# Macaron block with a blocked tanh scan: four scan steps issued elsewhere, the first normalisation and the add of eps on VectorE, one wait fewer

## The chip, the cores and the metric

The kernel runs on one core of a Trainium2 chip. The metric is the device time of one execution in microseconds (us); the time before is the median of three runs. A row of the trace names its engine as PE (TensorE matmuls), PEld (TensorE weight loads), DVE (VectorE), ACT (ScalarE), POOL (GpSimd) or SP (SyncE, which only issues DMAs here); a "q" behind it (PEldq, POOLq) is that engine's sequencer, which handles waits and register arithmetic. Ln is line n of the kernel.

## The reference: what is computed

The input x is 8 sequences of 512 tokens with 128 features. Half a feed-forward block is added, then a scan, then half the same feed-forward block again:

```python
def _L0_ffn_ref(x, ...):                        # hidden width 512
    h = silu(_tlin(x, w1_w, w1_s)) * _tlin(x, w2_w, w2_s)
    h = gelu(_tlin(h, h1_w, h1_s))
    h = gelu(_tlin(h, h2_w, h2_s))
    return _tlin(h, w3_w, w3_s)
...
def _L0_attn_ref(x, A, B, C, W_out, b_out):
    xB = einsum('bsd,dn->sbn', x, B)            # 16 states
    step: h = tanh(xb_t + h @ A.T)              # 512 steps in order
    return einsum('sbn,nd->bsd', hs, C) @ W_out.T + b_out
...
x = x + 0.5 * _L0_ffn_ref(_layernorm(x), ...)
x = x + _L0_attn_ref(_layernorm(x), ...)
x = x + 0.5 * _L0_ffn_ref(_layernorm(x), ...)
```

`_layernorm` subtracts the mean over the features and divides by sqrt(variance + 1e-5).

## The kernel before

**Tiling.** The 4096 tokens are cut into 8 chunks of 512 columns. Each chunk goes through the feed-forward block twice, so there are 16 passes, numbered g = 0 to 15. A pass has four layers; layer 2 and layer 3 are 512 by 512. Each float32 operand that moves through TensorE is split into a high part and a low part (`y_hi`, `y_lo`), so that each product is two matmuls of 128x512 with the same weights. Layer 2 and layer 3 have four output tiles m, each summed over four k: eight matmuls each.

**The scan.** The 512 steps of a sequence are done as 8 blocks side by side, so a chunk carries 8 steps t = 0 to 7 for 32 columns. One step is a short loop over three engines: TensorE does one matmul of 128x32 (`scan_step` of the tensor block, L437, which reads the state `h`), ScalarE does two tanh (L1232, L1233), and VectorE takes the low part of the state (`scan_low`, L856), which releases the next step's matmul through the semaphore `step_h`.

**The turns.** One turn does layer 2, 3 and 4 of pass g, layer 1 of pass g + 1, and the eight scan steps of another chunk between them. There are four kinds: the first turn (g = 0), early turns (g = 1 to 5, with steps from g = 3), middle turns (g = 6 to 8, in which the steps stand closer together in the second half) and turns (g = 9 to 14; 9 to 13 with steps), then a last turn. Passes 4 and 5 and passes 10 to 13 run in loops, so that their waits compare with registers (the order of instructions shows such register work as REGISTER_ALU or ISA). In the trace the early turn 2 lies at 59 to 83 us, the middle turn 6 at 152 to 175, 7 and 8 at 175 to 223, turn 9 at 223 to 246 and the turns 10 to 13 at 246 to 336.

**The order.** Every engine's order of instructions is written out by hand, in five blocks of code, one for each engine. An engine goes through its own list strictly in order and waits for semaphores of the others. Nothing is scheduled by a tool.

**The statistics.** For every chunk VectorE computes mean and variance (`statistics`: four BN_STATS, a small MEMSET, four BN_AGGR into `mv_f` or `mv_m`). GpSimd then adds eps (`ve_f`, `ve_m`, L1481) and raises the sum to the power -0.5 (`rs_f`, `rs_m`, L1484), both in `inverse_std`. Then the tokens are normalised, four instructions of 128x128 each, by VectorE (`normalise`, L796, into `xnt_f` or `xnt_m`) or, in early turns, by ScalarE from `rs_f` and `nbias`. TensorE turns the result round with four transposes (`to_features`, L302). "f" is the normalisation in front of a feed-forward block, "m" that in front of the scan.

In a turn, VectorE's order around the change is: `attention` (writes `lnin`), `low1`, `front_stats`, `layer4` (L851, writes `x1c` in the first eight passes and `outb` in the later ones), step 0, step 1, `normalise`, `low` of layer 2, step 2. In the middle turns 7 and 8 `layer4` is followed by `normalise`, `middle_stats` and `low`, and TensorE reads `x1c` in `middle_tokens` (L282) between layer 2's m = 1 and m = 2.

**Waits.** `wait(pe, l4_out, g)` in `layer2` at m = 2 protects the bank that layer 4 used. `middle_tokens`, which stands ahead of it in early and middle turns, waits for `l4_out` to reach `mid + 1`, which is g in those turns.

Of the kernel before, what the change touches and what calls it, by code (L numbers as in the profile page):

```python
# [24 lines left out]
ALU = mybir.AluOpType  # L25
# [33 lines left out]
def build(nc, xT, xtok, w1T, w2T, h1T, h2T, w3T, scales, Ablk, Brep, CTrep, WoutT, ident_d, mask_d, outT):  # L59
    with ExitStack() as ctx:  # L60
# [208 lines left out]
        def _(pe):  # L269
# [67 lines left out]
            def layer2(g, m, gen, beside=lambda k: None, ks=range(KT)):  # L337
                if m == 0 and ks[0] == 0:
                    if isinstance(g, int) and g == 1:
                        pe.wait_ge(y3_hi_r, 1)  # L340
                    else:
                        pe.wait_ge(y1_r, 4 * g + 3)
                if m == 1:
                    wait(pe, y3_hi_r, 4 * g)
                if m == 2:
                    wait(pe, l4_out, g)
                for k in ks:
                    if m == 0:
                        pe.wait_ge(y1_hi_r[k], g + 1)
                        if k < KT - 1:  # L350
                            pe.wait_ge(y1_lo_r, (KT - 1) * g + k + 1)
                        else:
                            pe.wait_ge(y1_lo_last, g + 1)
                    mm = split_mm(B2[m][:, :], 2, k, m, y1_hi[:, k, :], y1_lo[:, k, :], k == 0, k == KT - 1, gen)
                    if k == KT - 1:
                        mm.then_inc(l2_mm, 1)
                    beside(k)
# [90 lines left out]
            def early_turn(g, gen, mid, scan):  # L448
# [17 lines left out]
                layer2(g, 2, gen)  # L466
# [7 lines left out]
                layer3(g, 0, gen)  # L474
                step(5)
# [156 lines left out]
            def turn(k, g, gen, att, scan, joined=True):  # L632
# [15 lines left out]
                step(1)  # L648
                layer2(g, 2, gen)
                step(2)  # L650
                to_features("f", xnt_f, FR, g + 1)
                layer2(g, 3, gen)
                step(3)
# [106 lines left out]
        def _(dve):  # L760
            def statistics(kind, g, tile, st, mv):
                for q in range(QT):
                    i = nc.vector.bn_stats(st[:, q, :], tile[:, q * P:(q + 1) * P])
                i.then_inc(bns[kind], 1)
                dve.wait_ge(bns[kind], g + 1)
                nc.vector.memset(spare[:, :], 0.0)
                for q in range(QT):
                    i = nc.vector.bn_aggr(mv[:, q, :], st[:, q, :])  # L768
                i.then_inc(var[kind], 1)

# [228 lines left out]
            def turn(k, g, att, scan, joined=True):  # L999
# [9 lines left out]
                step(0)  # L1009
                step(1)  # L1010
                normalise("f", g + 1, FR, mv_f, rs_f, xnt_f)
# [63 lines left out]
            i.then_inc(var["f"], 1)  # L1075
            dve.wait_ge(ld_sc, 16)
# [401 lines left out]
        def _(pool):  # L1478
            def inverse_std(kind, g, mv, ve, rs):
                pool.wait_ge(var[kind], g + 1)  # L1480
                pool.tensor_tensor(ve[:, :], mv[:, :, 1], epsc[:, :], ALU.add).then_inc(veps[kind], 1)  # L1481
                pool.wait_ge(veps[kind], g + 1)
                wait(pool, normed[kind], g)
                pool.tensor_tensor(rs[:, :], ve[:, :], mhalf[:, :], ALU.pow).then_inc(rstd[kind], 1)  # L1484
# [22 lines left out]
            def early_turn(g, mid):  # L1507
                inverse_std("f", g + 2, mv_f, ve_f, rs_f)
                bias(g + 2)
                inverse_std("m", mid, mv_m, ve_m, rs_m)  # L1510
                rest(g, True)

            def middle_turn(g, c):
                if c > 0:
                    inverse_std("f", g + 1, mv_f, ve_f, rs_f)
                inverse_std("m", g - 1, mv_m, ve_m, rs_m)
                rest(g, True)

            def turn(k, g):
                last = isinstance(k, int) and k == CHUNKS - 1  # L1520
                if not last:
                    inverse_std("f", g + 1, mv_f, ve_f, rs_f)
# [13 lines left out]
            inverse_std("f", 0, mv_f, ve_f, rs_f)  # L1536
# [8 lines left out]
            inverse_std("f", 1, mv_f, ve_f, rs_f)  # L1545
# [9 lines left out]
            inverse_std("f", 2, mv_f, ve_f, rs_f)  # L1555
# [12 lines left out]
            def round_(r):  # L1568
# [3 lines left out]
                else:  # L1572
                    inverse_std("f", gb + CHUNKS, mv_f, ve_f, rs_f)
# [108 lines left out]
```

## Time and profile before

| | |
|---|---|
| median of 3 runs | 384.46 us (384.4 to 384.72) |
| the profiled execution's own time | 385.06 us |
| its span, first to last instruction | 383.1 us |
| TensorE matmul busy | 376.4 us, 98% of the span, 1793 matmuls |
| TensorE weight loads busy | 300.2 us, 78% |
| VectorE busy | 279.7 us, 73% |
| ScalarE busy | 268.0 us, 70% |
| GpSimd busy | 163.9 us, 43% |
| granted TensorE clock | 1.000 over the whole span (the 2.4 GHz level) |
| DMA | 14.00 MB in the whole span |

The profiled execution took 0.60 us more than the median of the runs, and 1.96 us of it lie outside the span. The ends of matmuls are modelled in the profile, and neighbouring matmuls overlap in it; how fast TensorE really goes is read from the distance between the starts of neighbouring matmuls, and a late one is seen at its weight load, which in regular flow starts with the matmul ahead of it.

### The profile page before, as it was taken

How to read it: one execution, taken by the hardware profiler on the slowest of the kernel's cores; microseconds unless marked ns; L12 is line 12 of the kernel's file. 1: busy time of each engine (PE TensorE's matmuls, PEld its weight loads, DVE VectorE, ACT ScalarE, POOL GpSimd, SP SyncE). 2: the span in 40 equal slices, each digit the busy share in tenths (PEclk: the TensorE clock that was granted, in tenths of full speed). 3: DMA queues.
4: the chain of work that ended last, by engine and by line, in shares of the span. 5: the costliest groups of instructions: out<-in, count | busy, mean ns of one | idle time of the engine just before them, and what ended most of it. 6: DMA issues, size and time to landing. Idle time of an engine off the chain costs nothing.

```text
span 383.1 us, 6587 instructions
## 1 busy us (share of the span) xinstructions
PE 376.4 (98%) x1793; PEld 300.2 (78%) x1793; DVE 279.7 (73%) x724; ACT 268.0 (70%) x625; POOL 163.9 (43%) x156
## 2 busy tenths in 40 slices
PE   8999999999999999999999999999999999999995
PEld 6777777778878787878778788888888888887774
DVE  4878989896777677576868866776767677686713
ACT  3889595777858688576784767758576775757654
POOL 3555262655525355142551633525334352533421
PEclk9999999999999999999999999999999999999999
DMA  7920000000000000000001001010100101000001
GB/s 226 436 110 1 27 2 27 3 2 28 2 28 0 2 27 0 28 2 28 27 2 56 2 8 49 0 55 2 41 14 0 55 0 55 0 30 26 2 28 32
DMA packets 6365, 14.00 MB, mean 37 GB/s; under 512 B 1088, under 2 KB 2112, under 8 KB 6080
## 3 DMA queue, kind: packets, MB, share of 16 engines
q1 hardware_dynamic: 5328, 13.37, 9.1%
q10 hardware_dynamic: 1008, 0.29, 0.3%
q8 instruction: 12, 0.20, 0.2%
q14 instruction: 17, 0.14, 0.1%
HBM read 7.37 MB, written 2.10 MB: 25 GB/s over the span
## 4 chain that ended last, share of the span: by engine, by line
PE 85%; issue 7%; POOL 3%; ACT 3%; DVE 2%; POOLq 0%; DVEq 0%
PE F L274 66%; PE FR L274 7%; PE SC L491 2%; PE FR L302 2%; POOL y_lo L1489 1%; PE SC L422 1%; POOL y_lo L1495 1%; PE F L519 1%; ACT y_hi L1216 1%; PE FR L292 1%; PE SC L274 1%; PE MI L302 1%; ACT y L1213 1%; PE F L521 1%; PE MI L282 1%
## 5 line engine op out<-in xcount | busy, mean ns | idle before, releaser
L274 PE MATMUL F<-y_hi,w_hi 128*128 128x512 f32 (+1 forms) x484 | 196.6, 407 | 0.3 <-DVE y_lo L1045 0.2
L274 PE MATMUL F<-y_lo,w_hi 128*128 128x512 f32 (+1 forms) x484 | 188.6, 390 | 0.0
L274 PEld LDWEIGHTS F<-y_hi,w_hi 128*128 128x128 f32 x484 | 90.9, 188 | 20.7 <-issue 2.2
L1213 ACT ACTIVATE y<-F,sc 128x512 f32<-128x512 f32 x111 | 76.1, 686 | 41.3 <-PE F L274 40.1
L274 PEld LDWEIGHTS F<-y_lo,w_hi 128*128 128x128 f32 x484 | 91.2, 188 | 15.9
L837 DVE TENSOR_TENSOR y_lo<-y,y_hi 128x512 fp32r<-128x512 f32 x79 | 64.8, 821 | 39.2 <-ACT y_hi L1216 39.2
L1489 POOL TENSOR_TENSOR y_lo<-y,y_hi 128x512 fp32r<-128x512 f32 x48 | 66.7, 1398 | 59.1 <-DVE y_hi L824 48.5
L1495 POOL TENSOR_TENSOR y_lo<-y,y_hi 128x512 fp32r<-128x512 f32 x48 | 62.6, 1310 | 34.6 <-ACT y_hi L1216 34.4
L1216 ACT ACTIVATE y_hi<-F,sc 128x512 fp32r<-128x512 f32 x111 | 76.1, 685 | 0.0
L1232 ACT ACTIVATE h<-SC 128x32 fp32r<-128x32 f32 x96 | 18.8, 196 | 48.0 <-PE SC L437 46.8
L274 PE MATMUL F<-xn_hi,w_hi 128*128 128x512 f32 x118 | 49.5, 419 | 0.1
L807 DVE SCALAR_TENSOR_TENSOR u<-th,F 128x512 f32<-128x512 f32 x61 | 41.5, 681 | 7.0 <-ACT th L1195 7.0
L274 PE MATMUL F<-xn_lo,w_hi 128*128 128x512 f32 x118 | 46.3, 393 | 0.0
L1481 POOL TENSOR_TENSOR ve_f<-mv_f,epsc 128x4 f32<-128x4 f32 x16 | 3.2, 202 | 96.6 <-DVE mv_f L768 91.6
L817 DVE SCALAR_TENSOR_TENSOR y<-F,s12h,u 128x512 f32<-128x512 f32 x58 | 43.3, 747 | 1.6
L1195 ACT ACTIVATE th<-F,s1h 128x512 f32<-128x512 f32 x61 | 41.1, 689 | 3.2 <-PE F L274 2.4
L856 DVE TENSOR_TENSOR h<-SC,h 64x32 fp32r<-64x32 f32 x96 | 17.1, 178 | 19.0 <-ACT SC L1233 18.2
L274 PEld LDWEIGHTS F<-xn_hi,w_hi 128*128 128x128 f32 x118 | 22.1, 187 | 6.9 <-DVE y L817 1.3
L274 PEld LDWEIGHTS F<-xn_lo,w_hi 128*128 128x128 f32 x118 | 22.2, 189 | 3.4
L274 PE MATMUL FR<-y_hi,w_hi 128*128 128x512 f32 x60 | 24.0, 399 | 0.0
L274 PE MATMUL FR<-y_lo,w_hi 128*128 128x512 f32 x60 | 23.4, 390 | 0.0
L437 PEld LDWEIGHTS SC<-h,a_mix 128*128 128x128 f32 x95 | 17.8, 188 | 6.6 <-DVE h L856 2.9
(170 smaller groups left out, 439.6 us busy)
## 6 DMA issues: line engine op xcount, KB each, us to landing
x_all<-in_xT SPq DMA_DIRECT2D x1, 2048.0 KB, 16.1
x_all<-x1c SPq DMA_DIRECT2D x8, 256.0 KB, 2.3
x_all<-lnin SPq DMA_DIRECT2D x8, 256.0 KB, 2.2
out<-outb SPq DMA_DIRECT2D x7, 256.0 KB, 2.0
x_all<-in_xtok SPq DMA_DIRECT2D x1, 1536.0 KB, 12.0
w_raw<-in_h1T SPq DMA_DIRECT2D x2, 512.0 KB, 7.8
w_raw<-in_h2T SPq DMA_DIRECT2D x2, 512.0 KB, 9.3
x_all<-in_xtok SPq DMA_DIRECT2D x2, 128.0 KB, 3.2
```

The costliest lines, as they stand in the source:

```text
L274: mm = nc.tensor.matmul(out, wtile(w, layer, k, m), y, start=first and i == 0, stop=last and i == len(pairs) - 1)
L437: nc.tensor.matmul(SC[:, span(t)], a_mix[:, :], states, start=False, stop=True, skip_group_check=True).then_inc(step_mm, 1)
L807: nc.vector.scalar_tensor_tensor(out=u[:, m % 2, :], in0=th[:, m % 2, :], scalar=1.0, in1=l1_banks(g, m, late)[0][:, :], op0=ALU.add, op1= ...
L817: nc.vector.scalar_tensor_tensor(out=y1[:, m, :], in0=l1_banks(g, m, late)[1][:, :], scalar=s12h[:, m:m + 1], in1=u[:, m % 2, :], op0=ALU. ...
L837: nc.vector.tensor_tensor(y_lo[:, k, :], y[:, k, :], y_hi[:, k, :].bitcast(F32), ALU.subtract).then_inc(out_sem, 1)
L856: nc.vector.tensor_tensor(h[0:64, span(t)], SC[0:64, span(CSTEPS + t)], h[0:64, span(t)].bitcast(F32), ALU.subtract).then_inc(step_h, 1)
L1195: nc.scalar.activation(th[:, m % 2, :], l1_banks(g, m, late)[0][:, :], ACT.Tanh, scale=s1h[:, m:m + 1]).then_inc(th_r, 1)
L1213: nc.scalar.activation(y23[:, m, :], bankt[:, :], ACT.Gelu, scale=s)
L1216: nc.scalar.activation(y_hi[:, m, :], bankt[:, :], ACT.Gelu, scale=s).then_inc(hi_r, 1)
L1232: nc.scalar.activation(h[:, span(t)], SC[:, span(t)], ACT.Tanh)
L1489: pool.tensor_tensor(y1_lo[:, m, :], y1[:, m, :], y1_hi[:, m, :].bitcast(F32), ALU.subtract).then_inc(y1_lo_r if m < KT - 1 else y1_lo_las ...
L1495: pool.tensor_tensor(y_lo[:, k, :], y[:, k, :], y_hi[:, k, :].bitcast(F32), ALU.subtract).then_inc(out_sem, 1)
```

## The change

Five edits, with nothing changed in what is computed:

1. On TensorE, step 1 of a turn is issued after the first k of layer 2's tile m = 2 instead of ahead of that tile; step 3 after the third k of tile m = 3 instead of behind the tile.
2. On TensorE, step 5 of an early turn is issued after the third k of layer 3's first tile instead of behind it.
3. On VectorE, a turn's `normalise` stands between step 0 and step 1 instead of behind step 1.
4. VectorE adds eps itself at the end of `statistics`, for every chunk and both kinds; it waits for its own BN_AGGR (`var`) and for the last use of the old value (`rstd`). GpSimd's `inverse_std` only raises to the power.
5. In early turns the wait for `l4_out` in `layer2` at m = 2 is left out.

The four scan steps or stages that stand elsewhere are thus steps 1 and 3 of `turn` and step 5 of `early_turn` on TensorE, and step 1's states against the normalisation on VectorE.

```diff
@@ tensor block
-            def layer2(g, m, gen, beside=lambda k: None, ks=range(KT)):
+            def layer2(g, m, gen, beside=lambda k: None, ks=range(KT), taken=True):
...
-                if m == 2:
+                if m == 2 and taken:
                     wait(pe, l4_out, g)
@@ tensor block, early_turn
-                layer2(g, 2, gen)
+                layer2(g, 2, gen, taken=False)
...
-                layer3(g, 0, gen)
-                step(5)
+                layer3(g, 0, gen, lambda k: step(5) if k == 2 else None)
@@ tensor block, turn
-                step(1)
-                layer2(g, 2, gen)
+                layer2(g, 2, gen, lambda i: step(1) if i == 0 else None)
                 step(2)
                 to_features("f", xnt_f, FR, g + 1)
-                layer2(g, 3, gen)
-                step(3)
+                layer2(g, 3, gen, lambda i: step(3) if i == 2 else None)
@@ vector block, statistics
                 i.then_inc(var[kind], 1)
+                dve.wait_ge(var[kind], g + 1)
+                wait(dve, rstd[kind], g)
+                ve = ve_f if kind == "f" else ve_m
+                nc.vector.tensor_scalar(ve[:, :], mv[:, :, 1], EPS, None, ALU.add).then_inc(veps[kind], 1)
@@ vector block, turn
                 step(0)
+                normalise("f", g + 1, FR, mv_f, rs_f, xnt_f)
                 step(1)
-                normalise("f", g + 1, FR, mv_f, rs_f, xnt_f)
                 low(g, 1, y2_hi_r, y23, y2_hi, y2_lo, y2_lo_dve)
@@ gpsimd block
-            def inverse_std(kind, g, mv, ve, rs):
-                pool.wait_ge(var[kind], g + 1)
-                pool.tensor_tensor(ve[:, :], mv[:, :, 1], epsc[:, :], ALU.add).then_inc(veps[kind], 1)
+            def inverse_std(kind, g, ve, rs):
                 pool.wait_ge(veps[kind], g + 1)
                 wait(pool, normed[kind], g)
                 pool.tensor_tensor(rs[:, :], ve[:, :], mhalf[:, :], ALU.pow).then_inc(rstd[kind], 1)
```

TensorE's order in the looped turns (passes 10 to 13), first piece: the tile m = 2 of layer 2; the row with `a_mix` is step 1.

```order
 L274 MATMUL F<-y_hi,w_hi 128x512
 L274 MATMUL F<-y_lo,w_hi 128x512
-L56 REGISTER_ALU
-L437 MATMUL SC<-h,a_mix 128x32
-L274 MATMUL F<-y_hi,w_hi 128x512
-L274 MATMUL F<-y_lo,w_hi 128x512
+L274 MATMUL F<-y_hi,w_hi 128x512
+L274 MATMUL F<-y_lo,w_hi 128x512
+L56 REGISTER_ALU
+L437 MATMUL SC<-h,a_mix 128x32
 L274 MATMUL F<-y_hi,w_hi 128x512
 L274 MATMUL F<-y_lo,w_hi 128x512
```

Step 1 now has two matmuls of 512 columns more ahead of it, and step 2 two fewer between it and step 1.

The same loop, second piece, at the end of the tile m = 3 and the start of layer 1 (`xn_hi`); the row with `a_mix` is step 3.

```order
 L274 MATMUL F<-y_hi,w_hi 128x512
 L274 MATMUL F<-y_lo,w_hi 128x512
-L274 MATMUL F<-y_hi,w_hi 128x512
-L274 MATMUL F<-y_lo,w_hi 128x512
-L56 REGISTER_ALU
-L437 MATMUL SC<-h,a_mix 128x32
+L56 REGISTER_ALU
+L437 MATMUL SC<-h,a_mix 128x32
+L274 MATMUL F<-y_hi,w_hi 128x512
+L274 MATMUL F<-y_lo,w_hi 128x512
 L56 REGISTER_ALU x2
 L274 MATMUL F<-xn_hi,w_hi 128x512
```

Step 3 is issued two matmuls earlier and no longer stands next to layer 1's register waits.

VectorE's order in the same loop, before, from the statistics to the low part of layer 2:

```order
L768 BN_AGGR mv_f<-st_f 128x2 x4
L840 REGISTER_ALU
L848 REGISTER_ALU
L56 ISA
L851 ISA
L851 SCALAR_TENSOR_TENSOR outb<-F,s3h,x_all 128x512
L855 ISA
L856 TENSOR_TENSOR h<-SC,h 64x32
L855 REGISTER_ALU
L856 TENSOR_TENSOR h<-SC,h 64x32
L796 TENSOR_SCALAR xnt_f<-FR,mv_f,rs_f 128x128 x4
```

and of the change:

```order
L765 BN_AGGR mv_f<-st_f 128x2 x4
L770 TENSOR_SCALAR ve_f<-mv_f 128x4
L841 REGISTER_ALU
L849 REGISTER_ALU
L56 ISA
L852 ISA
L852 SCALAR_TENSOR_TENSOR outb<-F,s3h,x_all 128x512
L856 ISA
L857 TENSOR_TENSOR h<-SC,h 64x32
L797 TENSOR_SCALAR xnt_f<-FR,mv_f,rs_f 128x128 x4
L856 REGISTER_ALU
L857 TENSOR_TENSOR h<-SC,h 64x32
```

One small instruction is added behind the statistics, and the four instructions of the normalisation stand ahead of the second state.

## Rows read from the trace of the kernel before

**Rows 1.** The page's busy time, share of the span, instructions.

```profile
PE 376.4 (98%) x1793; PEld 300.2 (78%) x1793; DVE 279.7 (73%) x724; ACT 268.0 (70%) x625; POOL 163.9 (43%) x156
```

**Rows 2.** Waits: who waited for whom; us in total, times, longest us.

```profile
PEld SC L437 <- DVE h L856: 2.9, 12, 0.3
...
PEld F L274 <- DVE y L817: 1.3, 4, 0.5
```

**Rows 3.** Timeline of TensorE, turn 10: start us, us, instruction.

```profile
254.10 0.28 PE L437 MATMUL SC<-h,a_mix 128*128 128x32 f32 x1
254.22 0.47 PE L274 MATMUL F<-y_hi,w_hi 128*128 128x512 f32 x1
```

**Rows 4.** Timeline of the weight loads, turn 10, with idle time and releaser.

```profile
253.63 0.19 PEld L274 LDWEIGHTS F<-y_lo,w_hi 128*128 128x128 f32 x1
254.09 0.19 PEld L437 LDWEIGHTS SC<-h,a_mix 128*128 128x128 f32 x1 [0.27 <-DVE h L856]
...
255.93 0.19 PEld L437 LDWEIGHTS SC<-h,a_mix 128*128 128x128 f32 x1
256.22 0.31 PEld L302 LDWEIGHTS FR<-ident,xnt_f 128*128 128x128 f32 x3
```

**Rows 5.** Timeline of VectorE, turn 10.

```profile
252.88 0.28 DVE L768 BATCH_NORM_AGGREGATE mv_f<-st_f 128x2 f32<-128x6 f32 x3
253.19 0.75 DVE L851 SCALAR_TENSOR_TENSOR outb<-F,s3h,x_all 128x512 f32<-128x512 f32 x1
253.86 0.17 DVE L856 TENSOR_TENSOR h<-SC,h 64x32 fp32r<-64x32 f32 x1
254.71 0.18 DVE L856 TENSOR_TENSOR h<-SC,h 64x32 fp32r<-64x32 f32 x1 [0.68 <-ACT SC L1233]
254.82 1.35 DVE L796 TENSOR_SCALAR xnt_f<-FR,mv_f,rs_f 128x128 f32<-128x128 f32 x4
```

**Rows 6.** Timeline of GpSimd, turn 10.

```profile
253.25 0.20 POOL L1481 TENSOR_TENSOR ve_f<-mv_f,epsc 128x4 f32<-128x4 f32 x1 [6.31 <-DVE mv_f L768]
253.61 1.01 POOL L1484 TENSOR_TENSOR rs_f<-ve_f,mhalf 128x4 f32<-128x4 f32 x1 [0.16 <-POOL ve_f L1481]
```

**Rows 7.** VectorE's small instruction `nmean`, all six (ns min/median/max).

```profile
L786 DVE TENSOR_SCALAR nmean<-mv_f x6: 170/170/171, 11.9 to 135.7; 128x4 f32<-128x4 f32 x6
```

**Rows 8.** Timeline of TensorE behind step 3, turn 9 and turn 10.

```profile
236.16 0.18 PE L437 MATMUL SC<-h,a_mix 128*128 128x32 f32 x1
...
236.51 0.40 PE L274 MATMUL F<-xn_lo,w_hi 128*128 128x512 f32 x1
...
258.57 0.18 PE L437 MATMUL SC<-h,a_mix 128*128 128x32 f32 x1
...
258.99 0.40 PE L274 MATMUL F<-xn_lo,w_hi 128*128 128x512 f32 x1
```

**Rows 9.** Timelines of GpSimd, VectorE and weight loads, early turn 2.

```profile
68.89 1.53 POOL L1484 TENSOR_TENSOR rs_m<-ve_m,mhalf 128x4 f32<-128x4 f32 x1 [0.22 <-POOL ve_m L1481]
70.39 2.54 POOL L1495 TENSOR_TENSOR y_lo<-y,y_hi 128x512 fp32r<-128x512 f32 x2
...
68.86 0.69 DVE L837 TENSOR_TENSOR y_lo<-y,y_hi 128x512 fp32r<-128x512 f32 x1
72.39 1.09 DVE L837 TENSOR_TENSOR y_lo<-y,y_hi 128x512 fp32r<-128x512 f32 x1 [0.57 <-ACT y_hi L1216]
...
74.92 0.19 PEld L274 LDWEIGHTS F<-xn_hi,w_hi 128*128 128x128 f32 x1 [0.51 <-DVE y L817]
```

**Rows 10.** Timelines of VectorE, weight loads and TensorE, middle turn 8.

```profile
206.58 0.72 DVE L851 SCALAR_TENSOR_TENSOR x1c<-F,s3h,x_all 128x512 f32<-128x512 f32 x1
...
207.35 0.48 PEld L282 LDWEIGHTS MI<-ident,x1c 128*128 128x128 f32 x4 [0.15 <-DVE x1c L851]
...
207.25 0.40 PE L274 MATMUL F<-y_lo,w_hi 128*128 128x512 f32 x1
207.48 0.60 PE L282 MATMUL MI<-ident,x1c 128*128 128x128 f32 x4
```

More of the change, by code:

```diff
@@ L1075, in _ @@
             i.then_inc(var["f"], 1)
+            dve.wait_ge(var["f"], 1)
+            nc.vector.tensor_scalar(ve_f[:, :], mv_f[:, :, 1], EPS, None, ALU.add).then_inc(veps["f"], 1)
             dve.wait_ge(ld_sc, 16)
@@ L1507, in early_turn @@
             def early_turn(g, mid):
-                inverse_std("f", g + 2, mv_f, ve_f, rs_f)
+                inverse_std("f", g + 2, ve_f, rs_f)
                 bias(g + 2)
-                inverse_std("m", mid, mv_m, ve_m, rs_m)
+                inverse_std("m", mid, ve_m, rs_m)
                 rest(g, True)
@@ L1514, in middle_turn @@
                 if c > 0:
-                    inverse_std("f", g + 1, mv_f, ve_f, rs_f)
-                inverse_std("m", g - 1, mv_m, ve_m, rs_m)
+                    inverse_std("f", g + 1, ve_f, rs_f)
+                inverse_std("m", g - 1, ve_m, rs_m)
                 rest(g, True)
@@ L1521, in turn @@
                 if not last:
-                    inverse_std("f", g + 1, mv_f, ve_f, rs_f)
+                    inverse_std("f", g + 1, ve_f, rs_f)
                 rest(g, not last)
@@ L1535, in _ @@
             pool.wait_ge(set_up, 1)
-            inverse_std("f", 0, mv_f, ve_f, rs_f)
+            inverse_std("f", 0, ve_f, rs_f)
             pool.wait_ge(normed["f"], 1)
@@ L1544, in _ @@
                 pool.tensor_tensor(part[0], part[1], part[2].bitcast(F32), ALU.subtract).then_inc(w_lo1_ready, 1)
-            inverse_std("f", 1, mv_f, ve_f, rs_f)
+            inverse_std("f", 1, ve_f, rs_f)
             bias(1)
@@ L1554, in _ @@
                                    ALU.subtract).then_inc(w_lo_ready, 1)
-            inverse_std("f", 2, mv_f, ve_f, rs_f)
+            inverse_std("f", 2, ve_f, rs_f)
             for k in (0, 2):
@@ L1572, in round_ @@
                 else:
-                    inverse_std("f", gb + CHUNKS, mv_f, ve_f, rs_f)
+                    inverse_std("f", gb + CHUNKS, ve_f, rs_f)
                     layer1(gb + CHUNKS)
```

## The prediction, made before the change was run

> **What bounds the kernel now.** I read the busy times first: TensorE's matmuls fill 376.4 of 383.1 us, at a granted clock of 1.000, and no other engine comes near [rows 1]. So an edit gains only where TensorE still waits. The view of waits says where: weight loads of scan steps wait for `h` twelve times, 2.9 us in total, and in the early turns four loads of layer 1 wait for the gated `y`, 1.3 us in total, 0.5 at the longest [rows 2]. That is idle time of weight loads, not of matmuls. In regular flow a load starts with the matmul ahead of it and neighbouring matmuls start 0.23 us apart (207.25 to 207.48), so a load may be late and cost nothing. In turn 8 the load of `x1c` idles 0.15 us, yet the matmul starts on time at 207.48 [rows 10]. In turn 10 step 1's load is due at 253.63 + 0.23 = 253.86 and comes at 254.09, 0.23 late; the next large matmul starts 0.12 behind step 1's small one [rows 3, 4], where about 0.03 is usual (my reading of the same timeline elsewhere, the floor of what a step can cost), so 0.09 is lost. I therefore price lateness at (late - 0.13), not below 0: 0.23 gives 0.10, near the 0.09. All sums below use it.
>
> **Step 1, turns 10 to 13.** The state of step 0 comes at 253.86 + 0.17 = 254.03, because `scan_low` stands behind `outb`, 253.19 to 253.94 [rows 5]. Two matmuls further on, step 1's load is due at 253.86 + 0.46 = 254.32. The added eps on VectorE delays `outb` and so the state by under 0.2 (below), to 254.2 or so: on time. Gain 0.09 in each of four turns.
>
> **The normalisation and step 2, turns 10 to 13.** This is where I expect the gain to go. Before, step 1's state is done at 254.71 + 0.18 = 254.89, long before step 2's load at 255.93 [rows 4, 5]. After, it stands behind `normalise`, which takes 1.35 us [rows 5] and cannot start before the power is done. The power starts at 253.61, 0.16 behind the end of GpSimd's add (253.25 + 0.20), and takes 1.01, to 254.62 [rows 6]. An add of eps on VectorE is not in this trace; its nearest row is `nmean`, the same form on 128x4, 0.17 us in all six cases [rows 7]. It waits for the aggregation's end, 252.88 + 0.28 = 253.16, so it runs from about 253.20 to 253.38. The way from VectorE to GpSimd's start is between 0.08 (aggregation's end 253.16 to GpSimd's add 253.25) and about 0.20 (the 0.16 between its two own instructions, and a little): the power starts at 253.45 to 253.57, ends at 254.46 to 254.58, and `normalise` starts at 254.50 to 254.61. The next instruction can start 1.28 behind it (`y_lo` does in this turn, as I read the timeline), so step 1's state starts at 255.78 to 255.89 and is done, with 0.18, at 255.96 to 256.07. Step 2's load is due at 255.93 less the 0.09 won ahead of it, 255.84. It is 0.12 to 0.23 late, and with a semaphore's way of some 0.05 up to 0.28: it costs 0 to 0.15. The transposes behind it, whose load stands at 256.22 because it waits for `xnt_f` until 254.82 + 1.35 = 256.17 [rows 4, 5], find `xnt_f` ready at 255.85 to 255.96 and are bounded by step 2's load instead. Those 0.29 us behind step 2 hardly shrink: step 2's load at 256.03 or so plus 0.19 is again 256.22. So step 1's gain is given back at step 2, or equally at the transposes: 0 for the first half of the turn, with bounds of -0.09 and +0.10 each.
>
> **Step 3, turns 10 to 13.** From step 3's matmul to layer 1's second matmul it is 236.51 - 236.16 = 0.35 us in turn 9, which is written out, and 258.99 - 258.57 = 0.42 in turn 10, a loop pass [rows 8]; there the order shows two register operations between the small matmul and layer 1. With step 3 two matmuls earlier they stand behind a matmul of 512 columns, which covers them. Gain 0.07 x 4 = 0.28. In turn 9 and the early turns nothing is there to gain from such a move, so step 5's move and the doubled wait, register work alone beside loads that are on time, stand at 0. Were the next state then late, step 4 has layer 1 as cover in both orders.
>
> **Early turns.** GpSimd's power for `rs_m` takes 1.53 us at 68.89 instead of the 1.01 of [rows 6], beside VectorE's `y_lo` from 68.86; its pair of `y_lo` follows at 70.39 and ends at 72.93, VectorE's `y_lo` at 72.39 takes 1.09 instead of 0.69, and the load of layer 1 is at last late by 0.51 - 0.04, about 0.47 [rows 9]: it costs 0.34. After, the power starts about 0.2 before 68.86, escapes that `y_lo`, the pair ends about 0.47 earlier, and VectorE's `y_lo` takes at least 0.3 less. I take 0.30, with bounds 0.07 (only the earlier start) and 0.34 (no lateness left). The Trainium skill, "SBUF — State Buffer", section "Who interferes with whom", says that VectorE and GpSimd share one port pair under an exclusive lock; the 1.53 and the 1.09 agree [rows 9]. Taken strictly it would move the wait to VectorE's `y_lo`, held until the power's end near 69.7, which nothing waits for until 70.4: the same 0.30. The other three late loads have together 0.8 us of idle time [rows 2] and mostly wait for ScalarE's chain, which the edit shortens only by what the power starts earlier: -0.07 in all.
>
> **Middle turns.** Here the edit harms. In turns 7 and 8 `x1c` follows the statistics at once (206.58) and its load already idles 0.15 [rows 10], which uses up the free lateness. The add, with its wait for the aggregation's end, pushes it by 0.15 to 0.24, as `outb` by 253.38 - 253.19 = 0.19 [rows 5]: cost 0.20 each. Some is got back since the same power starts earlier later in the turn; I take 0.06: +0.14 x 2 = +0.28. Turn 6 has one state pushed behind an added instruction, +0.07. The Trainium skill, "VectorE: DVE Perf Modes", "The DRAIN you can't avoid", says that a semaphore adds nothing to the gap between two operations. By it the add would cost only its start distance, near 0.1, and the middle turns +0.15 instead of +0.35.
>
> **Turns 9 and 14** have the normalisation of [rows 5] without a loop or without scan steps: -0.10 together. At the start the matmuls that TensorE does first are longer than the chain to `rs_f`: 0.
>
> **Sum.** -0.28 (step 3) + 0 (step 1, step 2, transposes) - 0.30 - 0.07 (early) + 0.28 + 0.07 (middle) - 0.10 = -0.40 us. Against the profiled execution's 385.06 that is 384.66; the median of the runs is 0.60 lower, 384.46, which gives 384.06, or 384.1.
>
> **Rivals.** A measurement of this kernel can tell about 0.2%, 0.77 us, from no change, so "same" is 383.69 to 385.23.
> (A) Faster: step 2 isn't late. If the power starts at 253.4 and `normalise` at 254.45, the state is done at 255.9 and inside the free lateness. Then the turns 10 to 13 gain the 0.09 of step 1, 0.05 at the transposes and 0.07 at step 3, 0.21 x 4 = 0.84, and with -0.30, -0.07, -0.10 and a milder +0.15 it is -1.16: 383.3. For it: the bounds above touch it. Against it: 1.35 us between a power and a state needs nearly every step at its lower bound.
> (B) Slower: the second states wait longer than I think behind `normalise`. It decides once `normalise` starts at 254.8 or later, that is, when the power doesn't start earlier at all, because the cross-engine way is longer than the one saved. Then the state comes at 256.26, 0.42 + 0.05 late, cost 0.34, less the 0.09, +0.25 in five turns, and the middle turns 0.24 each beyond: 1.25 + 0.48 + 0.07 - 0.28 - 0.07 = +1.45, 385.9. Against it: the add on VectorE takes 0.17 instead of 0.20 + 0.16.
> (C) Only the loops' register waits count less than I think and the early chain doesn't shorten: then -0.07 from the early turns, -0.10, 0 from step 3, +0.35: +0.18, 384.6. For it: 0.07 in [rows 8] is a difference between two places.
>
> **Chances.** Forecast 0.50, C 0.19, A 0.22, B 0.09. Forecast and C lie within 0.2%, but the forecast's lower bounds (0.09 x 4 more) reach 383.7, so some of it counts as faster: faster 0.26, same 0.63, slower 0.11. The range reaches from most of A to beyond C: 383.2 to 384.9; what is left out is B and the end of A.
>
> **What would show it.** In turn 10: step 1's load with no idle time for `h`, then step 2's load with 0.1 to 0.3 idle for `h` (if none, A; if 0.4 or more, B); `rs_f` starting 0.05 to 0.15 earlier against the aggregation; from step 3's matmul to the second one behind it 0.35, and regular steps of 0.23 from there into layer 1. In turn 2: the power at 1.0 and layer 1's load late by less than 0.2. In turns 7 and 8: `x1c`'s load idle by 0.3 to 0.4. I am wrong if the state behind `normalise` isn't TensorE's next wait, or if the added 0.17 costs far more in statistics that I took for covered.

## The result, and the profile after

The changed kernel takes 385.77 us (median of 6, 385.56 to 386.36) against 384.43 us of the kernel before in the same session: ratio 1.004, 95% interval 1.0027 to 1.0053. It is 1.3 us slower, where a gain was forecast (384.1 us, range 383.2 to 384.9).

The page's busy times, share of the span and instructions of the changed kernel, beside [rows 1]:

```profile
PE 376.3 (98%) x1793; PEld 298.5 (78%) x1793; DVE 283.7 (74%) x748; ACT 268.6 (70%) x625; POOL 158.5 (41%) x132
```

The waits of the changed kernel (who waited for whom; us in total, times, longest us), beside [rows 2]:

```profile
PEld F L274 <- DVE outb L852: 2.8, 6, 0.6
PEld SC L437 <- DVE h L857: 2.2, 10, 0.3
...
PEld F L274 <- DVE y L818: 1.1, 4, 0.4
...
PEld MI L282 <- DVE x1c L852: 1.0, 2, 0.5
```

The waits for `h` and `y` are still there. Large weight loads now wait for `outb`, which none did before, 0.6 us at the longest, and the load of `x1c` waits 0.5 where it waited 0.15 [rows 10].

**Where the time went.** TensorE executes the same 1793 matmuls in both kernels, so the start of matmul number n after, less that before, is the time lost up to there. This table takes it by part of the program; the rows on the turns 10 to 13 are means over the four. Two experiments below show how fine it reads. e3 and e11 have no effect, and differ from the kernel before by up to 0.07 in the turns 6 to 8, by 0.14 in all, and by 0.01 in a mean over the turns 10 to 13.

| part of the program | after less before, us |
|---|---|
| start-up, to matmul 250 | -0.84 |
| turn 2 to turn 5 | -0.41 |
| middle turns 6 to 8 | +0.49 |
| turn 9 | 0.00 |
| turns 10 to 13, each: up to step 2 | +0.32 |
| turns 10 to 13, each: step 2 and the transposes | -0.07 |
| turns 10 to 13, each: from there into layer 1 | +0.10 |
| turn 14 and last turn | +0.04 |
| all behind start-up | +1.53 |

The start-up part differs by anything from -1.2 to 0 among the thirteen profiles of changed kernels, edits there or not (-0.98 in one that changes nothing ahead of turn 1, e11), so it is left out: it is why the two profiled executions, 385.56 and 385.06 us, stand only 0.5 apart. The +1.53 behind it goes with the 1.34 between the medians.

Timeline of the weight loads, turn 10, of the changed kernel (start us, us, instruction, idle time and releaser), beside [rows 4]:

```profile
252.87 0.19 PEld L274 LDWEIGHTS F<-y_lo,w_hi 128*128 128x128 f32 x1
253.64 0.19 PEld L274 LDWEIGHTS F<-y_hi,w_hi 128*128 128x128 f32 x1 [0.59 <-DVE outb L852]
253.75 0.19 PEld L274 LDWEIGHTS F<-y_lo,w_hi 128*128 128x128 f32 x1
253.99 0.19 PEld L437 LDWEIGHTS SC<-h,a_mix 128*128 128x128 f32 x1
...
255.49 0.19 PEld L437 LDWEIGHTS SC<-h,a_mix 128*128 128x128 f32 x1
255.72 0.42 PEld L302 LDWEIGHTS FR<-ident,xnt_f 128*128 128x128 f32 x4
...
258.23 0.19 PEld L274 LDWEIGHTS F<-xn_hi,w_hi 128*128 128x128 f32 x1 [0.32 <-issue]
```

Timeline of VectorE, same turn, beside [rows 5]:

```profile
252.25 0.15 DVE L765 BATCH_NORM_AGGREGATE mv_f<-st_f 128x2 f32<-128x6 f32 x1
252.44 0.17 DVE L770 TENSOR_SCALAR ve_f<-mv_f 128x4 f32<-128x4 f32 x1
252.84 0.75 DVE L852 SCALAR_TENSOR_TENSOR outb<-F,s3h,x_all 128x512 f32<-128x512 f32 x1 [0.23 <-issue]
253.51 0.17 DVE L857 TENSOR_TENSOR h<-SC,h 64x32 fp32r<-64x32 f32 x1
253.81 1.37 DVE L797 TENSOR_SCALAR xnt_f<-FR,mv_f,rs_f 128x128 f32<-128x128 f32 x4
255.09 0.17 DVE L857 TENSOR_TENSOR h<-SC,h 64x32 fp32r<-64x32 f32 x1
```

Timeline of TensorE, same turn, at tile m = 2, beside [rows 3]:

```profile
253.10 0.40 PE L274 MATMUL F<-y_lo,w_hi 128*128 128x512 f32 x1
253.65 0.50 PE L274 MATMUL F<-y_hi,w_hi 128*128 128x512 f32 x1
253.99 0.40 PE L274 MATMUL F<-y_lo,w_hi 128*128 128x512 f32 x1
254.23 0.18 PE L437 MATMUL SC<-h,a_mix 128*128 128x32 f32 x1
254.25 0.47 PE L274 MATMUL F<-y_hi,w_hi 128*128 128x512 f32 x1
```

The first load of tile m = 2 is due at 253.10 and comes at 253.64, when `outb` is written (252.84 + 0.75 = 253.59). The matmul starts 0.55 behind its neighbour instead of 0.23, and the next one 0.34. Step 1, behind it, and step 2 find their states in time: their loads have no idle time. On VectorE the aggregation ends at 252.25 + 0.15 = 252.40 and `outb` starts at 252.84, 0.44 later; before it was 0.03 (253.16 to 253.19 in [rows 5]). Of these 0.44 the add takes 0.17; the rest is a gap of 0.04 ahead of the add and 0.23 behind it, for which the profile names no releaser (e6 and e7 explain it). The normalisation starts 1.41 us behind the aggregation's end, where the prediction had 1.34 to 1.45, and was 1.66 before.

Timeline of VectorE and of the weight loads, turn 8, of the changed kernel, beside [rows 10]:

```profile
205.37 0.28 DVE L765 BATCH_NORM_AGGREGATE mv_f<-st_f 128x2 f32<-128x6 f32 x3
205.68 0.17 DVE L770 TENSOR_SCALAR ve_f<-mv_f 128x4 f32<-128x4 f32 x1
205.86 0.75 DVE L852 SCALAR_TENSOR_TENSOR x1c<-F,s3h,x_all 128x512 f32<-128x512 f32 x1
...
206.67 0.42 PEld L282 LDWEIGHTS MI<-ident,x1c 128*128 128x128 f32 x4 [0.48 <-DVE x1c L852]
```

The same aggregation in the kernel before, on VectorE's timeline:

```profile
206.39 0.28 DVE L768 BATCH_NORM_AGGREGATE mv_f<-st_f 128x2 f32<-128x6 f32 x3
```

It ended at 206.67, and `x1c` started at 206.58 [rows 10], 0.09 ahead of that end; now it starts 0.21 behind it (205.65 to 205.86). In this turn, which isn't in a loop, the delay is 0.30, in turn 10 it is 0.44 less 0.03, 0.41.

### The profile page after: what moved, and what is told of

Read it like the earlier page. It is cut to its first block, busy times and chain, and to the rows that moved or that the text cites. A ratio compares the mean times of both kernels' runs of the same rounds, so it can differ in the third digit from the quotient of the medians.

```text
span 383.7 us, 6609 instructions
## 1 busy us (share of the span) xinstructions
PE 376.3 (98%) x1793; PEld 298.5 (78%) x1793; DVE 283.7 (74%) x748; ACT 268.6 (70%) x625; POOL 158.5 (41%) x132
## 4 chain that ended last, share of the span: by engine, by line
PE 92%; DVE 2%; ACT 2%; DMA 1%; issue 1%; POOL 0%; SPq 0%; DVEq 0%; POOLq 0%
PE F L274 72%; PE FR L274 8%; PE FR L302 2%; DMA w_raw<-in_w2T 1%; PE F L527 1%; PE SC L422 1%; PE MI L282 1%; PE F L518 1%; PE MI L302 1%; PE FR L292 1%; PE SC L274 1%; DVE outb L852 1%; DVE st_f L760 1%; PE F L520 1%; ACT y_hi L1219 1%
## 5 line engine op out<-in xcount | busy, mean ns | idle before, releaser
L838 DVE TENSOR_TENSOR y_lo<-y,y_hi 128x512 fp32r<-128x512 f32 x79 | 63.9, 808 | 45.9 <-ACT y_hi L1219 45.9
L1485 POOL TENSOR_TENSOR rs_f<-ve_f,mhalf 128x4 f32<-128x4 f32 x16 | 16.1, 1009 | 98.7 <-DVE ve_f L770 78.2
L1203 ACT CAST y_hi<-y 128x512 fp32r<-128x512 f32 x34 | 21.0, 618 | 2.6 <-DVE y L818 2.6
```

Source lines behind the costliest of these rows:

```text
L838: nc.vector.tensor_tensor(y_lo[:, k, :], y[:, k, :], y_hi[:, k, :].bitcast(F32), ALU.subtract).then_inc(out_sem, 1)
L1203: nc.scalar.copy(y1_hi[:, m, :], y1[:, m, :]).then_inc(y1_hi_r[m], 1)
```

## The experiments

Theory 1: the loss is what the add of eps does on VectorE. It waits for the aggregation's end, and what is queued behind it, `outb`, `x1c`, the state of step 0 and, in loops, their register operations, comes later, and TensorE waits for whichever it meets first. Theory 2: the loss comes with step 1's move, since step 1's wait had covered the wait for `outb` at tile m = 2. The tables give TensorE's loss against the kernel before, in us, by the parts above.

| kernel | t2-5 | t6-8 | t9 | t10-13, each: to step 2 | transposes | into layer 1 | all behind start-up | median, of this / before |
|---|---|---|---|---|---|---|---|---|
| changed | -0.41 | +0.49 | 0.00 | +0.32 | -0.07 | +0.10 | +1.53 | 385.77 / 384.43 |
| e1 add alone | -0.37 | +0.59 | +0.12 | +0.41 | 0.00 | +0.01 | +2.08 | 385.81 / 384.11 |
| e2 step 1 alone | 0.00 | 0.00 | +0.43 | -0.07 | +0.46 | -0.01 | +1.98 | 386.40 / 384.11 |
| e3 step 3 alone | -0.03 | -0.07 | -0.05 | 0.00 | +0.01 | 0.00 | -0.14 | 384.36 / 384.11 |
| e4 all but the add | -0.03 | -0.07 | +0.06 | -0.09 | +0.30 | -0.02 | +0.75 | 385.08 / 384.11 |
| e5 add behind layer4 | -0.47 | +1.15 | +0.50 | -0.09 | +0.87 | -0.02 | +4.65 | 389.33 / 383.96 |
| e6 dummy, with wait | -0.39 | +0.59 | +0.15 | +0.41 | 0.00 | 0.00 | +2.03 | 386.01 / 383.96 |
| e7 dummy, no wait | +0.05 | +0.16 | -0.01 | +0.01 | 0.00 | 0.00 | +0.25 | 385.22 / 383.96 |
| e8 early add, state first | -0.59 | 0.00 | -0.06 | -0.05 | -0.05 | +0.07 | -0.77 | 383.36 / 383.96 |
| e9 step 1 back | -0.43 | +0.54 | +0.01 | +0.42 | -0.08 | +0.08 | +1.83 | 386.50 / 384.67 |
| e10 normalise alone | +0.01 | +0.06 | +0.04 | 0.00 | +0.21 | -0.01 | +0.95 | 385.51 / 384.67 |
| e11 early edits alone | +0.02 | +0.07 | -0.02 | +0.01 | 0.00 | +0.01 | +0.14 | 383.78 / 384.67 |
| e12 state, add, outb | -0.51 | +0.03 | -0.09 | +0.22 | -0.07 | +0.08 | +0.37 | 384.64 / 384.67 |

e5, e6, e7, e9, e10 and e11 have a single time each, whose start-up part can be off by 1 us; they are read by the parts. The others have ratios 1.0042 (1.0030 to 1.0055) for e1, 1.0059 (1.0046 to 1.0072) for e2, 1.0004 (0.9994 to 1.0014) for e3, 1.0026 (1.0015 to 1.0037) for e4, 0.998 (0.9969 to 0.9991) for e8 and 1.000 (0.999 to 1.001) for e12.

**e1, the add alone** (edit 4, nothing else).

> Only the add of eps moved to VectorE (edit 4), TensorE's order untouched. Theory 1, the add itself is the cost: in the loop turns it stands, with a wait of its own, between the aggregation and outb, and outb starts 0.4 us behind the aggregation's end where it was 0.03; step 0's state follows outb, so step 1's weight load, 0.23 late before, becomes 0.6 late and costs 0.4 to 0.5 more in each of turns 10 to 13 (+1.6 to +2.0), x1c costs +0.5 in turns 7 and 8 together, and turn 2 gives back 0.34: in all +1.5 to +2.2 us over the turns. Theory 2, the cost is that step 1 stood in front of the bank's wait in layer 2's tile m = 2 and covered it: without that move the add costs only the 0.5 of the middle turns less the 0.34, in all 0 to +0.4 us. Theory 3, this is start-up: no difference inside the turns.

Theory 1's sizes, +0.41 a turn and +2.08 in all. Theory 2 is out: with step 1 still in front of tile m = 2 the price is larger than in the changed kernel, not absent.

**e2, step 1 alone.**

```diff
-                step(1)
-                layer2(g, 2, gen)
+                layer2(g, 2, gen, lambda i: step(1) if i == 0 else None)
```

> Only step 1 moved behind the first k of tile m = 2. Theory 1: outb ends at the old time, 0.08 us behind the moment at which tile m = 2's first weight load is due, so that load is late by about 0.13 and costs next to nothing, step 1's own lateness (0.09 a turn) is gone, but a late load and the small matmul now each pay their own slower next matmul (0.08 to 0.11): -0.05 to +0.1 a turn, in all -0.2 to +0.4 us. Theory 2: the exposed bank wait alone costs 0.3 a turn: +1.2 us in turns 10 to 13.

Both theories missed it. At tile m = 2 it is a gain of 0.07, near theory 1's best case. The exposed wait is there, 0.2 us at the longest in this kernel's waits, but costs nothing. At the transposes 0.46 is lost, and their load in turn 10 says why. First the wait, then the weight load:

```profile
PEld F L274 <- DVE outb L850: 0.7, 4, 0.2
...
256.41 0.42 PEld L302 LDWEIGHTS FR<-ident,xnt_f 128*128 128x128 f32 x4 [0.57 <-DVE xnt_f L795]
```

VectorE's normalisation stands behind step 1's state there, which now comes later, and `xnt_f` with it. So moving step 1 calls for edit 3, which takes a part of this back: e4, which has both, loses 0.30 there.

**e3, step 3 alone.**

```diff
-                layer2(g, 3, gen)
-                step(3)
+                layer2(g, 3, gen, lambda i: step(3) if i == 2 else None)
```

> Only step 3 moved behind the third k of tile m = 3. As the prediction had it: the register operations of layer 1 are covered by a large matmul, -0.07 in each of turns 10 to 13, -0.28 us. As the changed kernel's trace suggests (layer 1's first load 0.32 idle with no releaser): the register operations stand in TensorE's sequencer where nothing covers them wherever the step is, and apart from the small matmul they pay a second slow start: +0.07 to +0.10 in each of four turns, +0.3 to +0.4 us.

Neither size: nothing in the turns 10 to 13. Layer 1's first load follows VectorE's `xn_lo`, not step 3. VectorE and the weight loads of the kernel before, and then of e3, in turn 10:

```profile
257.74 0.69 DVE L802 TENSOR_TENSOR xn_lo<-FR,xn_hi 128x512 fp32r<-128x512 f32 x1 [0.87 <-ACT xn_hi L1190]
...
258.66 0.19 PEld L274 LDWEIGHTS F<-xn_hi,w_hi 128*128 128x128 f32 x1
```

```profile
257.46 0.69 DVE L801 TENSOR_TENSOR xn_lo<-FR,xn_hi 128x512 fp32r<-128x512 f32 x1 [0.86 <-ACT xn_hi L1189]
...
258.38 0.19 PEld L274 LDWEIGHTS F<-xn_hi,w_hi 128*128 128x128 f32 x1 [0.24 <-issue]
```

The load stands 0.23 behind the end of `xn_lo` both times (258.43 to 258.66, 258.15 to 258.38), and in the changed kernel too (258.00 to 258.23). Two register operations lie between, and they carry the waits: in e3 they start at 258.19 and 258.29, behind the end of `xn_lo`, which is why the profile says "issue". In the turns 9 and 14 of the changed kernel, which are written out, the load follows `xn_lo` by 0.05. So the register operations do cost about 0.17 in the loop, as the prediction supposed, but they run only when `xn_lo` is done, and no matmul issued ahead of them can cover them, wherever step 3 is.

**e4, all edits but the add.**

> All edits but the add of eps: steps 1, 3 and 5, the normalisation ahead of step 1's state, the dropped wait. Theory 1: most of the loss is gone: turns 7 and 8 as before, turn 2 without its gain, turns 10 to 13 at about +0.1 to +0.2 each (step 3's and the bank wait's own slow start): +0.3 to +0.8 us against before, 0.8 to 1.2 below the changed kernel. Theory 2: turns 10 to 13 keep their +0.3 each: +1.3 us.

+0.75, inside theory 1's range, but the place isn't the one expected: tile m = 2 gains 0.09, as the prediction had it, and 0.30 is lost at step 2 and the transposes, the part of the turn where the forecast had counted on an earlier power. Step 2's load in turn 10 of e4:

```profile
255.94 0.19 PEld L437 LDWEIGHTS SC<-h,a_mix 128*128 128x128 f32 x1 [0.36 <-DVE h L853]
```

**e5, the add behind layer4 in turns and middle turns.**

```diff
-                front_stats(g + 1)
+                front_stats(g + 1, False)
                 if joined:
                     layer4(1, g - 1, k - 1)
+                add_eps("f", g + 1, mv_f)
                 step(0)
```

> The changed kernel with the add of eps still on VectorE but behind layer4 (outb or x1c) in the turns and the middle turns. Theory 1, the cost is what the add does to outb and x1c: the 0.30 to 0.33 us lost at tile m = 2 in each of turns 10 to 13 is gone (-0.08 against before, as without the add), turns 7 and 8 are at 0 instead of +0.26 and +0.22; but the power starts about 0.4 us later against the aggregation than before, so the normalisation is late and 0.4 to 0.7 is lost at the transposes. Theory 2, the added instruction costs wherever it stands on VectorE: tile m = 2 keeps its +0.3.

The loss at tile m = 2 is gone (-0.09), so the instruction costs nothing at this tile where it doesn't stand in front of `outb`. The late power costs 0.87 at step 2 and the transposes, more than expected, because it starts 1.01 behind the aggregation's end (254.36) and not 0.4 but 0.56 later than before (0.45 there, 253.16 to 253.61 in [rows 5, 6]); 0.56 on top of the 0.30 of e4, whose normalisation stands in the same place, makes 0.86. Timeline of GpSimd, turn 10 of e5:

```profile
255.37 1.01 POOL L1491 TENSOR_TENSOR rs_f<-ve_f,mhalf 128x4 f32<-128x4 f32 x1 [7.25 <-DVE ve_f L774]
```

In turns 7 and 8 the load of `x1c` waits no longer than before (0.2 at most), but the late `rs_f` costs 0.56 each there.

**e6 and e7, an unused instruction behind each aggregation**, GpSimd adding as before.

```diff
                 i.then_inc(var[kind], 1)
+                dve.wait_ge(var[kind], g + 1)
+                nc.vector.tensor_scalar(extra[:, :], mv[:, :, 1], EPS, None, ALU.add)
```

In e7 the wait is left out, and the instruction reads the constant `epsc`. Nothing else is computed otherwise.

> The kernel before, GpSimd still adding eps, with one more instruction on VectorE behind each aggregation, same form and operand as the add and with the same wait for the aggregation's end, its result unused. Theory 1, displacement: the same losses as with the add alone, +0.42 at tile m = 2 in each of turns 10 to 13, +0.27 and +0.28 in turns 7 and 8, +0.12 in turn 9, and no gain in turn 2 beyond 0.1. Rival: the loss comes with the power's new timing; then these are near 0.

> As the last, but the additional instruction reads a constant and waits for nothing. Theory 1a, what costs is the wait, which also uncovers the queue's register operations behind it: outb starts only about 0.07 us later, turns 10 to 13 lose 0.05 to 0.1 each, turns 7 and 8 under 0.1. Theory 1b, any instruction of 0.17 us there costs its whole time: 0.2 or more in each turn.

e6 repeats the losses of the add alone part by part, +0.41 and +2.03 against +0.41 and +2.08. e7 costs 0.01 in each of the turns 10 to 13, less than both theories had, and +0.25 in all, where e3 and e11, which have no effect, differ by 0.14. Timelines of VectorE in turn 10, first e6, then e7:

```profile
252.33 0.17 DVE L772 TENSOR_SCALAR extra<-mv_f 128x4 f32<-128x4 f32 x1
252.74 0.75 DVE L854 SCALAR_TENSOR_TENSOR outb<-F,s3h,x_all 128x512 f32<-128x512 f32 x1 [0.23 <-issue]
```

```profile
252.73 0.28 DVE L769 BATCH_NORM_AGGREGATE mv_f<-st_f 128x2 f32<-128x6 f32 x3
252.92 0.14 DVE L771 TENSOR_SCALAR extra<-epsc 128x4 f32<-128x4 f32 x1
253.04 0.75 DVE L853 SCALAR_TENSOR_TENSOR outb<-F,s3h,x_all 128x512 f32<-128x512 f32 x1
```

With no wait the additional instruction slips in and `outb` starts 0.03 behind the aggregation's end, as before. With the wait VectorE's queue stops at it, and the four register operations that form the waits of `outb`, of 40 to 64 ns each, are worked off only behind it. VectorE's queue in turn 10 of the changed kernel, by line (ns min/median/max, start us), and then two of the same four in the kernel before:

```profile
L841 DVEq ALU_OP  x1: 40/40/40, 252.4 to 252.4; - x1
...
L849 DVEq ALU_OP  x1: 50/50/50, 252.5 to 252.5; - x1
...
L56 DVEq FUSED_REGOPS  x1: 46/46/46, 252.6 to 252.6; - x1
...
L852 DVEq FUSED_REGOPS  x1: 64/64/64, 252.7 to 252.7; - x1
```

```profile
L840 DVEq ALU_OP  x1: 40/40/40, 252.8 to 252.8; - x1
...
L851 DVEq FUSED_REGOPS  x1: 64/64/64, 253.1 to 253.1; - x1
```

The trace's own start times place them closer. Before, the four run from 252.80, 0.01 behind the start of the first of the four aggregations, to 253.15, and in e7 from 252.65 to 252.99, so the aggregations cover them. In the changed kernel they run from 252.45, 0.01 behind the start of the add, to 252.79, and in e6 from 252.35 to 252.69. In all four kernels they take 0.34 to 0.35 us with the gaps between them, and `outb` starts 0.05 behind the last. That accounts for the whole 0.44 of the changed kernel: 0.03 from the aggregation's end to the add, 0.01 to the first register operation, 0.34 for the four and 0.05 to `outb`; the add's own 0.17 runs beside them. In turn 8, outside a loop, there are no register operations, and `x1c` starts 0.01 behind the add's end (205.85 to 205.86).

e6 and e7 differ in the operand as well as in the wait. No run changes one of them alone; but in both `outb` starts 0.05 behind the last register operation, so it is their place that sets its start.

Surprising in e6: it has turn 2's gain as well (-0.39), although its power isn't early against the statistics. The part on the prediction takes that up.

**e9, the changed kernel with step 1 back in front of tile m = 2.**

> The changed kernel with step 1 back in front of tile m = 2. Theory 1, the late outb and the late state of step 0 cost TensorE the same 0.3 to 0.4 whichever of the two it meets first: tile m = 2 loses 0.42 in each of turns 10 to 13, as with the add alone, instead of 0.31, so this kernel is slower than the changed one by 0.1 a turn. Theory 2, the move uncovered the wait: tile m = 2 near 0, 1.2 us faster than the changed kernel.

+0.42 there instead of +0.32: theory 1's number. The move saves 0.1 a turn of a loss that the add makes.

**e10, the normalisation alone ahead of step 1's state.**

```diff
                 step(0)
+                normalise("f", g + 1, FR, mv_f, rs_f, xnt_f)
                 step(1)
-                normalise("f", g + 1, FR, mv_f, rs_f, xnt_f)
```

> Only the normalisation ahead of step 1's state. It starts when the power is done, 0.16 earlier than before, and step 1's state comes behind it, about 256.1 in the time of turn 10, so step 2's load is 0.25 late and costs about 0.1, and the transposes behind it another 0.1: +0.1 to +0.25 in each of turns 10 to 13. If the state's order didn't matter, these would be 0 or -0.05.

+0.21 at step 2 and the transposes, as expected. Weight loads, turn 10:

```profile
255.96 0.19 PEld L437 LDWEIGHTS SC<-h,a_mix 128*128 128x128 f32 x1 [0.27 <-DVE h L856]
```

**e11, step 5's move and the dropped wait alone.**

> Only step 5 of an early turn moved and the wait for the bank in early turns left out. Both theories: no turn differs by more than 0.05 us, because the loads there are on time in the kernel before.

Turn 2 to turn 5 differ by 0.02, as expected. No effect of these edits can be told from none.

**e8 and e12, attempts at a better kernel.** Both leave TensorE's order as before, put the add on VectorE in the early turns, and take step 0's state ahead of `outb`:

```diff
                 front_stats(g + 1)
+                step(0)
                 if joined:
                     layer4(1, g - 1, k - 1)
-                step(0)
```

e12 also has the add in turns 9 to 14, between that state and `outb`.

> The kernel before with the add of eps on VectorE in the early turns alone, and step 0's state ahead of outb on VectorE in turns 9 to 13, nothing else. Theory 1: turn 2 keeps its -0.37 to -0.41; in turns 10 to 13 step 1's load is on time and the bank's wait behind it late by 0.1 at most: -0.09 each at tile m = 2, half of it given back at the transposes, which wait for the normalisation: in all -0.5 to -0.8 us against before, 383.3 to 383.6 beside 384.1. Rival: the state isn't there yet at that place (ScalarE's tanh is late) and holds outb up: +0.1 or more a turn.

> The version with step 0's state first and the add on VectorE in early turns, and now the add in turns 9 to 14 too, between step 0's state and outb. Theory 1a, the wait for the aggregation's end is covered by the state, but the register operations behind the add are not covered by its 0.17 us: outb starts 0.2 to 0.35 us later than without the add, is late for its bank's wait behind step 1, and costs 0.1 to 0.2 in each of turns 10 to 13; the power is about 0.1 earlier, worth 0.05 at the transposes: +0.2 to +0.6 us in all against the version without it. Rival: with the wait covered the add costs only itself, and the earlier normalisation makes it 0.2 us faster than that version.

e8 is faster than the kernel before, 383.36 against 383.96 us (theory 1 had 0.5 to 0.8), where the changed kernel is 1.3 slower. Nearly all of it is the add in the early turns: -0.59 in turns 2 to 5. In the turns 10 to 13 step 1's load is in time. Of the 0.05 won there and the 0.05 at the transposes, 0.07 is given back on the way into layer 1, so the state's new place is worth some 0.03 a turn; that edit wasn't run alone. e12 takes the gain away, 384.64 against 384.67 us: by the parts it loses 0.26 more than e8 in each of the turns 10 to 13, more than the 0.1 to 0.2 expected. The state covers the aggregation's end, but the register operations still follow the add, and `outb` starts 0.41 behind the add's start. Timeline of VectorE, turn 10 of e12:

```profile
252.31 0.15 DVE L864 TENSOR_TENSOR h<-SC,h 64x32 fp32r<-64x32 f32 x1
252.43 0.17 DVE L777 TENSOR_SCALAR ve_f<-mv_f 128x4 f32<-128x4 f32 x1
252.84 0.75 DVE L859 SCALAR_TENSOR_TENSOR outb<-F,s3h,x_all 128x512 f32<-128x512 f32 x1 [0.24 <-issue]
```

## Why the prediction was wrong

**The step that failed** is "Step 1, turns 10 to 13": "The added eps on VectorE delays `outb` and so the state by under 0.2 (below), to 254.2 or so: on time. Gain 0.09 in each of four turns." It failed twice. The delay is 0.41 (e6), because I priced an instruction and not what a wait does to the queue behind it. And I followed only the state that comes behind `outb`, not `outb` itself: with step 1 moved, the first instruction that needs VectorE is the first load of tile m = 2, whose wait for `l4_out` stands in the section on the kernel. Its moment is 0.46 us before step 1's new one. The prediction's own price, lateness less 0.13, fits once both are put right (an estimate): the load is due at 253.86, and `outb`'s old end 253.94 with 0.41 and a semaphore's 0.05 makes 0.54 late, 0.41 less the 0.09 won at step 1, +0.32, which is what was measured. With the forecast's delay of 0.19 it would have been +0.10, and with the state alone followed next to nothing.

The forecast's 0 for this half of the turn (0.09 won, given back at step 2) measured +0.32 - 0.07 = +0.25 in each of the four turns, 1.0 us. It is the largest part of the 1.93 us between the forecast sum (-0.40) and the +1.53; the way into layer 1 (+0.10 for -0.07, four times) makes 0.68, the middle turns 0.14, turns 9 and 14 together 0.14, and the early turns take 0.04 back. Of the two edits that meet here the add is the one that costs: without it the part gains 0.09 or 0.07, although the wait for `outb` is exposed (e4, e2), and without the move the add costs 0.41 or 0.42 (e1, e9).

**The normalisation and step 2** were right in mechanism and start (1.41 us behind the aggregation), but the price was never called in, because TensorE was 0.3 late by then. So step 2's load had no idle time, which I had named as rival A's sign, without A's gain. Where TensorE isn't late, e4 and e10 show the price, with +0.30 and +0.21 for 0 forecast with 0.10 as a bound: my bounds took the add's earlier power for granted, and without it the state is later.

**Step 3**, -0.28, measured 0.00 (e3). The 0.07 of [rows 8] is register work, but it stands behind the end of `xn_lo` and not beside the small matmul, so a matmul of 512 columns can't cover it. In the changed kernel the 0.07 won at the transposes is lost again on the way into layer 1, because its first load follows `xn_lo`; e12, with step 3 in its old place, shows the same (-0.07 and +0.08). What the changed kernel loses beyond that, 0.02 to 0.03, isn't explained.

**Early turns**, -0.37 forecast, -0.41 measured; the way was another. The power does escape VectorE's `y_lo`, but an earlier power isn't needed for that: the added instruction also makes `y_lo` start later, and in e6, whose power stands where it stood against the statistics, that alone gives the gain. In the changed kernel both moved, by 0.22 each; whether the earlier power alone would do, no run shows. Timelines of GpSimd and VectorE in turn 2, the changed kernel, then e6, then e7:

```profile
67.82 1.01 POOL L1485 TENSOR_TENSOR rs_m<-ve_m,mhalf 128x4 f32<-128x4 f32 x1 [0.38 <-DVE ve_m L770]
...
68.24 0.68 DVE L838 TENSOR_TENSOR y_lo<-y,y_hi 128x512 fp32r<-128x512 f32 x1
```

```profile
67.67 1.01 POOL L1487 TENSOR_TENSOR rs_m<-ve_m,mhalf 128x4 f32<-128x4 f32 x1 [0.22 <-POOL ve_m L1484]
...
67.87 0.69 DVE L840 TENSOR_TENSOR y_lo<-y,y_hi 128x512 fp32r<-128x512 f32 x1
```

```profile
68.52 1.60 POOL L1486 TENSOR_TENSOR rs_m<-ve_m,mhalf 128x4 f32<-128x4 f32 x1 [0.20 <-POOL ve_m L1483]
...
68.57 0.69 DVE L839 TENSOR_TENSOR y_lo<-y,y_hi 128x512 fp32r<-128x512 f32 x1
```

Before, `y_lo` started 0.03 ahead of the power, 68.86 and 68.89, and the power took 1.53 [rows 9]. Starting first doesn't save the power: in e7 it starts 0.05 ahead and takes 1.60, and e7 has no gain in turn 2. A power that is held ends 0.87 behind the end of `y_lo` (69.55 and 70.42 before, 69.26 and 70.12 in e7); as it takes 1.01 alone, it seems to need what `y_lo` holds about 0.14 after its start (an estimate, 1.01 less 0.87). In e6 `y_lo` comes 0.20 behind the power's start, and nothing is held up. The Trainium skill, "SBUF — State Buffer", section "Who interferes with whom", calls the shared port pair an exclusive lock; the trace agrees for a power that meets a running `y_lo` and doesn't for the `y_lo` behind a power that started first, which takes its usual 0.69 in e6 and in e7. In the changed kernel the early add brings the same collision to the turns 3, 4, 5, 7 and 8, whose powers take 1.38 to 1.45 instead of 1.01 (at 90.21, 113.36, 136.68, 185.44 and 209.84); it cost TensorE nothing there that the table can tell.

**Middle turns**, +0.35 forecast, +0.49 measured: turns 7 and 8 lost 0.26 and 0.22 where I had 0.20 less 0.06. `x1c` came 0.30 later instead of 0.15 to 0.24, since it had been slipped in ahead of the aggregation's end, and turn 6 lost nothing where I had 0.07. The Trainium skill, "VectorE: DVE Perf Modes", "The DRAIN you can't avoid", has a semaphore cost nothing between two operations, measured on equal copies. Here an instruction of the same form costs 0.01 us of TensorE's time a turn without a wait and 0.41 with one (e7, e6): the trace disagrees where the wait uncovers the register operations of the instruction behind.

**The dropped wait and step 5**, 0 forecast, 0.02 measured (e11). **Start-up**, 0 forecast; its spread hides anything smaller than 1 us.

**The rivals.** B named 385.9, near the measured 385.77, but by another mechanism: it needed a power that starts no earlier and a late step 2, and both were not so. Only its 0.48 for the turns 7 and 8 is what they lost; its time was right by accident. A is refuted: turn 10 lost where it had a gain. C was right that step 3 gains nothing, which e3 shows, and wrong on the early turns (-0.41 for its -0.07) and on the time, 384.6.

What stays open: what sets the start-up's spread, and whether the add with its wait would be harmless in a loop without the four register operations. They are timed in the trace, and turn 8 has none, but they weren't taken out of a loop alone.

## What to carry to other kernels

Price a new instruction on an engine by what its wait does to the queue behind it, register operations included, and by the first consumer of each thing queued there, not by its 0.17 us. When a stage is moved away from in front of a tile, list every wait of the instruction that becomes the first one there: a wait that was always covered by its neighbour has no row in the trace of before. Here it cost nothing while `outb` came on time, and it was where TensorE met the late one. And take edits apart before judging them: here the add alone gained 0.4 us in the early turns and lost 2.5 elsewhere (e1), and keeping it only where it gained, with the state ahead of `outb`, gave the one version that is faster.

## What the runs showed that I had not expected

- One small instruction with a wait on the instruction just ahead delays its successor by 0.41 us in a loop and 0.30 outside one; an instruction of the same form without the wait, in the loop, delays it by nothing.
- VectorE's queue works off the register operations of a wait while the instructions ahead are still executing, until it meets a wait: the four of `outb` stand beside the aggregations in the kernel before and behind the add in the changed one.
- Behind a late or a small matmul the next one is slow once, 0.31 to 0.34 us instead of 0.23. In e1, where the late one is step 1's small matmul, that happens once; in the changed kernel's tile m = 2, where the late one and step 1 are apart, twice (0.34 and 0.31).
- Some 0.15 us decide on 0.5 us: GpSimd's power takes 1.60 when VectorE's two-input subtraction starts 0.05 behind it and 1.01 when it starts 0.20 behind.
